# The low parts of the second layer's second four gated units, on GpSimd instead of VectorE

## The reference, cut to what matters

```
xn = _layernorm(x)
x = x + _L1_attn_ref(xn, weight_qkv, weight_out) + _L1_ffn_ref(xn, w_gate, w_up, w_down)
```

```
h = silu(xn @ w_gate) * (xn @ w_up)          # 1024 hidden columns
h_sparse = _sparsify_2to4(h)                 # of each group of 4, the 2 largest in magnitude stay
return h_sparse @ w_down
```

## Time and profile before

| | us |
|---|---|
| median of 3 runs | 727.8 (727.42, 727.8, 854.93) |
| the profiled execution's own time | 727.74 |
| its span, first to last instruction | 725.7 |
| PE busy | 688.8 (95%) |
| PEld busy | 582.6 (80%) |
| DVE busy | 519.1 (72%) |
| ACT busy | 373.4 (51%) |
| POOL busy | 138.1 (19%) |

### The profile page before, as it was taken

How to read it: one execution, slowest core, us unless ns; L and a number is a source line. 1 busy time by engine, 2 the same in 40 slices (tenths; PEclk the granted TensorE clock), 3 DMA queues, 4 the chain that set the end, 5 groups by cost and what they waited for, 6 DMA issues and landing times.

```text
span 725.7 us, 10583 instructions
## 1 busy us (share of the span) xinstructions
PE 688.8 (95%) x4030; PEld 582.6 (80%) x4030; DVE 519.1 (72%) x936; ACT 373.4 (51%) x769; POOL 138.1 (19%) x128
## 2 busy tenths in 40 slices
PE   3899999889999999999999999999898999999997
PEld 2768888778878788887888878887676888888886
DVE  6626566984966567565675656757768998998996
ACT  5786777554744425454254443446555455354541
POOL 7543453610000010000100001000040323303220
PEclk9989999999999999999999999999999999999999
DMA  5085443000000000000000000050000000000000
GB/s 188 5 281 194 135 141 100 1 1 1 0 1 1 0 1 1 1 1 0 1 1 1 0 1 1 1 233 0 1 1 0 1 1 30 1 29 1 2 30 30
DMA packets 21282, 25.78 MB, mean 36 GB/s; under 512 B 976, under 2 KB 19408, under 8 KB 20464
## 3 DMA queue, kind: packets, MB, share of 16 engines
q1 hardware_dynamic: 20576, 23.79, 9.7%
q10 hardware_dynamic: 656, 1.31, 0.5%
HBM read 22.94 MB, written 2.16 MB: 35 GB/s over the span
## 4 chain that ended last, share of the span: by engine, by line
PE 69%; DVE 20%; issue 5%; ACT 4%; POOL 2%; DMA 1%; DVEq 0%; POOLq 0%
PE bank L89 21%; PE bank L91 19%; PE bank L90 19%; DVE l_ring_lo L2411 3%; DVE l_ge L2392 2%; DVE l_h L2407 2%; PE bank L488 2%; DVE l_o L2415 1%; DVE h_raw L1147 1%; DVE fused_lo L141 1%; POOL m_den L817 1%; DVE l_h L2364 1%; PE bank L1465 1%; PE bank L464 1%; DVE m_st L893 1%
## 5 line engine op out<-in xcount | busy, mean ns | idle before, releaser
L1147 DVE TENSOR_TENSOR h_raw<-h_s,bank 128x512 f32<-128x512 f32 x104 | 71.4, 687 | 116.8 <-ACT h_s L1137 102.3
L1137 ACT ACTIVATE h_s<-bank 128x512 f32<-128x512 f32 x104 | 62.1, 597 | 164.5 <-PE bank L91 164.4
L1152 DVE TENSOR_TENSOR h_ring_lo<-h_raw,h_ring_hi 128x512 fp32r<-128x512 f32 x92 | 68.9, 749 | 0.0
L1141 ACT ACTIVATE h_ring_hi<-h_raw 128x512 fp32r<-128x512 f32 x104 | 64.7, 622 | 0.2 <-DVE h_raw L1147 0.2
L90 PE MATMUL bank<-fused_lo,h_ring_hi 128*128 128x256 f32 x208 | 58.2, 280 | 0.0
L89 PE MATMUL bank<-l_xT_hi,l_wgu 128*128 128x512 f32 x128 | 51.9, 406 | 2.6 <-DVE l_h L2364 2.6
L2112 ACT ACTIVATE l_s<-bank 128x512 f32<-128x512 f32 x32 | 19.1, 598 | 66.4 <-PE bank L91 66.4
L89 PE MATMUL bank<-f_yT_hi,mlp_hi 128*128 128x512 f32 x128 | 51.1, 400 | 0.6 <-DVE h_raw L1147 0.4
L90 PE MATMUL bank<-l_xT_lo,l_wgu 128*128 128x512 f32 x128 | 50.9, 397 | 0.0
L91 PE MATMUL bank<-l_xT_hi,l_lo 128*128 128x512 f32 x128 | 50.7, 396 | 0.0
L91 PE MATMUL bank<-f_yT_hi,fused_lo 128*128 128x512 f32 x128 | 50.0, 390 | 0.0
(11 more groups left out here) (355 smaller groups left out, 2023.5 us busy)
## 6 DMA issues: line engine op xcount, KB each, us to landing
m_W<-m_scratch SPq DMA_DIRECT2D x16, 512.0 KB, 6.3
fused_raw<-in_fused SPq DMA_DIRECT2D x1, 3584.0 KB, 16.2
res<-in_x SPq DMA_DIRECT2D x4, 512.0 KB, 6.1
fused_raw<-in_fused SPq DMA_DIRECT2D x2, 1024.0 KB, 8.5
l_raw<-in_layer SPq DMA_DIRECT2D x1, 2048.0 KB, 8.8
out_x<-res SPq DMA_DIRECT2D x16, 128.0 KB, 1.9
l_raw<-in_layer SPq DMA_DIRECT2D x1, 1280.0 KB, 11.3
fused_raw<-in_fused SPq DMA_DIRECT2D x1, 1152.0 KB, 5.1
```

The lines of the kernel that those rows point to most:

```text
L1137: self.nc.scalar.activation(self.s[u % 2][r, :], gate[r, :], ACT.Silu).then_inc(self.silu.sem, 1)
L1141: self.nc.scalar.activation(self.unit(i, u)[0], self.product(i, u), ACT.Copy).then_inc(self.hi.sem, 1)
L1147: self.nc.vector.tensor_tensor(out=self.product(i, u), in0=self.s[u % 2][r, :], in1=up[r, :], op=ALU.mult).then_inc(self.hidden.sem, 1)
L1152: self.nc.vector.tensor_tensor(out=lo, in0=self.product(i, u), in1=f32(hi), op=ALU.subtract).then_inc(self.lo.sem, 1)
```

## The change

In the three steady tiles the low parts of units 4 to 7 are made by GpSimd instead of VectorE: a new function `low` in GpSimd's block, called four times between `products(i + 1)` for l = 0, 1 and for l = 2, 3. It waits for the unit's high part (`hi`), does the same subtraction from the same tensors into the same place, and counts up the same semaphore `lo`. VectorE's four calls are gone. Since two engines now count up `lo`, VectorE waits, before its first `low(i, 0, 0)` of tiles 1, 2 and 3, until all of the tile before are counted. The last tile's low parts stay on VectorE.

```diff
+        def low(i, c, j):
+            pool.wait_ge(hi.sem, hi.at(i, c * GP + j + 1))
+            nc.gpsimd.tensor_tensor(out=ring[j][1][:, :], in0=h[c][j][:, :], in1=f32(ring[j][0][:, :]), op=ALU.subtract).then_inc(lo.sem, 1)
+
...
         for i in range(C - 1):
             weigh(i)
-            products(i + 1)
+            products(i + 1, range(2))
+            for j in range(GP):
+                low(i, 1, j)
+            products(i + 1, range(2, L))
         weigh_last(C - 1)
...
                 for l in range(L - 1):
                     attended(i, l)
+                if i:
+                    dve.wait_ge(lo.sem, lo.at(i, 0))
                 low(i, 0, 0)
...
             else:
                 times(i, 7)
+                dve.wait_ge(lo.sem, lo.at(i, 0))
                 for j in range(GP):
                     low(i, 0, j)
...
                 low_o(i)
                 times(following, 1)
-                for j in range(GP):
-                    low(i, 1, j)
                 times(following, 2)
```

## The result

| | before | changed |
|---|---|---|
| median of 11 runs, us | 727.42 | 734.85 |
| ratio, 95% interval | | 1.0096 [1.0073, 1.0119] |
| the profiled execution's own time, its span, us | 727.74, 725.7 | 736.25, 734.5 |

One execution of each kernel stands far above the rest (854.93 and 766.58 us) and is left out of the ratio. By the bound of 2% this is no change; but the interval shows a loss of 5 to 9 us. The forecast was 733.6, a ratio of 1.008.

The account below looks back on a forecast made before the run. TensorE was taken to set the pace, with VectorE without slack ahead of low_o. Relief counted 0 and the collision 3 x 1.95 = 5.85 us, added to 727.74 us for 733.6 us; range 729.5 to 738.8.

Parts of the forecast that it names:

- What bounds the kernel: In the steady tiles TensorE sets the pace; VectorE has no slack ahead of low_o, so TensorE waits in full for additions.
- The relief valued at nothing: Taking four subtractions, 4.41 us, off VectorE behind low_o gains nothing, since TensorE doesn't wait there.
- GpSimd's price: One 512-element subtraction on GpSimd takes 1.3 us, with 1.06 and 1.53 as bounds.
- rival 5: Slower by over 2%: GpSimd's fp32r-writing subtraction is much slower than its f32 products; 743 us and more, chance 0.04.
- The collision: In each steady tile GpSimd's subtractions block VectorE's keeps of units 6 and 7, making low_o 1.95 us late.
- TensorE's gap: Ahead of attention_out in each steady tile, TensorE's idling for low_o grows from 0.26 to 2.2 us.
- rival 1: One block instead of two: the first subtraction comes after unit 6's keep; late by 1.15, 731.2 us, chance 0.15.
- Rival 3: No block: GpSimd's subtractions and VectorE's keeps don't meet, nothing changes; 727.7 us, chance 0.10.
- The rest on GpSimd: Later subtractions finish before downs(i, 1); the larger products end near 637.05 instead of 633.1, at no cost.
- the cover of 0.9: VectorE's reductions of the larger products end near 638.3, 0.9 us ahead of the silu that times(following, 3) needs at 639.15.
- Rival 2: Two blocks plus TensorE's clock at half behind the gap, 1.6 us lost in each of three tiles; 738.4 us, chance 0.14.
- the likeliest case: Two keeps blocked in each of three steady tiles, no slower clock: 733.6 us, chance 0.52.

Follow-up runs that it names:

- e5: Kernel before, VectorE still making all low parts, with GpSimd doing the four subtractions again into spare room nobody reads: 735.24 us, ratio 1.0112.
- e1: Changed kernel with GpSimd's four subtractions held until all of VectorE's keeps of the tile are done: 727.9 us, ratio 1.0016.
- e6: Changed kernel with the low parts of units 4 to 7 of the steady tiles made by nobody: 726.86 us, ratio 0.9992.
- e2: Changed kernel with the four subtractions behind both larger products in GpSimd's queue: 726.19 us, ratio 0.9993.
- e4: Changed kernel with low_o ahead of the keeps of units 6 and 7 in VectorE's queue: 727.27 us, ratio 0.9999.
- e9: Changed kernel with low_o ahead of the keeps of units 6 and 7, and tile 0's times of units 4 and 5 before the vote: 723.5 us.
- e12: Repeat of e8, kernel before with both moves of VectorE's order, on one chip with e9: 723.58 us, ratio 0.9972.
- e7: Changed kernel with subtractions behind both larger products, low_o before the keeps, tile 0's times of units 4 and 5 before the vote: 720.09 us.
- e8: Kernel before, all low parts on VectorE, with low_o before the keeps and tile 0's times of units 4 and 5 before the vote: 723.82 us.

## Why the prediction was right

**What bounds the kernel.** TensorE, and ahead of `low_o` VectorE with no slack: e5 and e1 show both sides of it. The relief valued at nothing: e6 (0.9992, nothing done) and e5 against the changed kernel (735.24 and 734.85, VectorE's load kept or taken off) agree. It holds for VectorE's order of before; with `low_o` first the relief has a price, 1.2 us.

**GpSimd's price.** 1.3 us was the estimate for a subtraction that isn't blocked; 1.27 is the shortest of the changed kernel and e1's four in 5.05 us make 1.26. The two full streams of the q and k products were the right neighbour; the 1.06 of the e and v products would have been wrong. The fp32r output of rival 5 cost nothing that shows in these.

**The collision.** Two keeps caught, 1.95 us forecast; 3.09 - 1.20 = 1.89 measured, in each of the three tiles. TensorE's gap: 2.2 forecast, 2.15 to 2.22 measured. The four subtractions ended 0.2 us after TensorE resumed, as forecast. The first subtraction came 0.45 us ahead of the keep (by the steps of the forecast 0.44; rival 1 spoke of some 0.3), so rival 1, one block, didn't happen in any tile of this profile. Rival 3, no block, is out.

**The rest on GpSimd.** The two larger products were forecast to end 637.05 - 632.57 = 4.5 us after TensorE resumes; they end at 640.42, 4.4 after 636.05. VectorE waited for them (6.8 us in six waits), and then still 1.0 us for the silu: the cover of 0.9 held.

**The clock.** Here the forecast was short by a part. Rival 2 put the fall in all three tiles or none; it came in two, at 1.5 us each instead of 1.6. Forecast 5.85 us for the gaps alone; the profile has 5.7 of gaps and 3.0 of clock, and the 11 runs by their ratio about 7.0 (0.0096 x 727.42). The truth lies between the likeliest case and rival 2, 733.6 and 738.4. The sum is right in mechanism and in its main term; the term left out is the clock, carried as a rival of all or nothing at 0.14, of which two tiles of three came true in this profile. That the median, 734.85, lies only 1.3 us above the forecast is in part luck: what the clock costs differs from execution to execution by more than that. TensorE was busy up to the gaps, as the case against rival 2 had it, and the clock fell behind two of them all the same.

## What to carry to other kernels

Ask of an instruction that is moved to an idle engine not only who waits for it, but what it shuts out while it runs: here 1.3 us on an engine busy 21% of the time stood on the path twice a tile, because VectorE's instructions beside it read two SBUF tensors. Where it must go there, hold it until these are done (e1), put it further back in its queue (e2), or take what TensorE waits for out of its reach (e4); beside instructions that read one tensor, or PSUM, it cost nothing. And before relieving a busy engine, leave its work out once (e6): that tells what the relief is worth in the order as it stands. It doesn't carry over to another order: e2 and e6 gained nothing, and with `low_o` first the same relief was worth 1.2 us. Where other waits hide it, close them and ask again.

## What the runs showed of the hardware

- When both want SBUF, VectorE (two inputs there) and GpSimd (reading) take turns, instruction by instruction, also where one has more in its queue: four subtractions against two keeps took 5.91 us instead of 5.05, the keeps 3.09 instead of 1.20. A scalar_tensor_tensor with a bf16 and an f32 input is shut out as a tensor_tensor is.
- Three gaps of 2.15 to 2.22 us in TensorE's work had different ends: the granted clock fell behind those of tiles 0 and 2 and not behind that of tile 1, in the same way in one profiled execution each of two programs (the changed kernel and e5: 0.71 and 0.70, 1.00 and 1.00, 0.57 and 0.56 in the first 3.0 to 3.2 us). What tells them apart no run shows.
- In the 35 runs of the kernel before that stand beside e9 to e12, nine had a clock of 0.998 over the span and took 722.7 to 723.0 us; the others had 0.990 to 0.995 and took 725.2 to 728.9. The same program differs by up to 6 us, for the most part with what TensorE's clock does, which is more than most of what is compared here; at one mean clock, 0.993, it still differs by 2.5 us. Medians of few runs that mix clocks mislead: e7's and e8's lie 3.7 us apart, of which their traces, both at full clock from tile 0 to the last tile, show 1.2.
